# Ids spread across partitions by matmuls, seven one-hots on ACT, and layer 1 summed in steps of two chunks

## The reference

```
e = stack([tbl_f[ids[:, f]] for f in range(40)], axis=1)       # 512 x 40 x 32
z = einsum('bpd,pde,bpe->bp', e[:, iidx], bilinear, e[:, jidx])  # 512 x 780
h = concatenate([z, dense_ctx], axis=1)                          # 512 x 796
h = maximum(h @ W_top1 + b_top1, 0)                              # 512
h = maximum(h @ W_top2 + b_top2, 0)                              # 256
y = h @ W_top3
```

## Time and profile before

| what | value |
|---|---|
| median of 3 runs (lowest, highest) | 208.79 us (207.69, 212.2) |
| the profiled execution | 208.05 us |
| its span, first to last instruction | 206.2 us |
| PE busy | 180.9 us (88%) |
| DVE busy | 152.6 us (74%) |
| POOL busy | 102.9 us (50%) |
| ACT busy | 28.3 us (14%) |
| mean granted clock of PE | 0.992 |

### The profile page before, as it was taken

One profiled execution on the slowest core, in us unless ns is written; L12 is line 12 of the kernel. 1 busy time (PEld: TensorE's weight loads), 2 busy tenths in 40 slices (PEclk: granted clock), 3 DMA queues, 4 the chain that ended last, 5 costly groups with the idle time before them and its releaser, 6 DMA issues.

```text
span 206.2 us, 3399 instructions
## 1 busy us (share of the span) xinstructions
PE 180.9 (88%) x1440; PEld 57.3 (28%) x1440; DVE 152.6 (74%) x153; ACT 28.3 (14%) x40; POOL 102.9 (50%) x110
## 2 busy tenths in 40 slices
PE   0097659569989999999999999999998999999993
PEld 0043213222322232222322333313223223322441
DVE  1588599996779899998458774989693967992502
ACT  2445310100111020011111021100102012001311
POOL 5787787877777777777777777000012020200000
PEclk9999999979999999999999999999999999999999
DMA  6999521130043929140000000000000000000000
GB/s 175 369 368 370 210 67 40 17 97 13 15 116 75 324 27 313 38 153 13 17 14 13 13 13 16 3 0 5 0 0 0 3 0 0 0 3 0 0 0 0
DMA packets 8039, 14.95 MB, mean 72 GB/s; under 512 B 2117, under 2 KB 4553, under 8 KB 8025
## 3 DMA queue, kind: packets, MB, share of 16 engines
q1 hardware_dynamic: 4952, 13.16, 18.8%
q0 software_dynamic: 3072, 1.58, 4.3%
HBM read 14.73 MB, written 0.00 MB: 71 GB/s over the span
## 4 chain that ended last, share of the span: by engine, by line
PE 65%; DVE 4%; issue 2%; DVEq 0%
PE ps_t L589 23%; PE ps_z L603 20%; PE ps_x L630 9%; PE ps_t L583 3%; DVE prod L519 3%; PE ps_t L640 3%; PE ps_t L616 2%; PE ps_x L565 2%; PE ps_x L616 1%; DVE prod L529 0%; PE ps_z L649 0%; DVE prod L532 0%; DVEq L518 0%; DVEq L528 0%
## 5 line engine op out<-in xcount | busy, mean ns | idle before, releaser
L519 DVE TENSOR_TENSOR prod<-ps_t,xt 128x1024 f32<-128x1024 f32 x100 | 115.2, 1215 | 30.1 <-PE ps_t L589 24.7
L426 POOL DMA_INDIRECT emb<-tbl,idx x96 | 96.7, 1007 | 30.1 <-issue 28.7
L589 PE MATMUL ps_t<-xt,w_sb 32*128 32x512 f32 x360 | 59.1, 640 | 0.0
L603 PE MATMUL ps_z<-prod,ones 128*32 128x512 f32 x400 | 53.1, 604 | 0.4 <-DVE prod L519 0.4
L589 PEld LDWEIGHTS ps_t<-xt,w_sb 32*128 32x128 f32 x360 | 20.2, 183 | 33.6 <-issue 23.3
L431 POOL TENSOR_TENSOR late_z<-late_z,tbl_oh 128x512 f32<-128x512 f32 x4 | 5.1, 1277 | 42.9 <-ACT tbl_oh L459 42.9
L482 DVE TENSOR_SCALAR hot<-ids,ramp 128x2048 bf16<-128x2048 f16 x34 | 23.7, 750 | 3.4 <-ACT ids L443 2.1
L553 PE MATMUL ps_x<-hot,tbl_oh 125*32 125x512 bf16 x72 | 8.7, 463 | 13.5 <-DVE hot L482 13.5
L630 PE MATMUL ps_x<-late_z,late_w 128*128 128x512 f32 x40 | 19.3, 613 | 0.0
L603 PEld LDWEIGHTS ps_z<-prod,ones 128*32 128x32 f32 x400 | 8.0, 108 | 39.2 <-issue 29.3
L583 PE MATMUL ps_t<-xt,w_sb 32*32 32x512 f32 x160 | 11.5, 634 | 2.7 <-ACT xt L448 1.9
(11 more groups left out here) (44 smaller groups left out, 68.3 us busy)
## 6 DMA issues: line engine op xcount, KB each, us to landing
late_z<-ids_oh SPq DMA_DIRECT2D x8, 512.0 KB, 7.3
tbl_oh<-small_tables SPq DMA_DIRECT2D x3, 512.0 KB, 6.0
emb<-tbl,idx POOLq DMA_INDIRECT x96, 2.3
late_w<-w SPq DMA_DIRECT2D x1, 1024.0 KB, 7.4
late_w<-w SPq DMA_DIRECT2D x1, 768.0 KB, 6.8
w_sb<-w_pairs SPq DMA_DIRECT2D x1, 704.0 KB, 4.0
tbl_oh<-small_tables SPq DMA_DIRECT2D x1, 640.0 KB, 9.3
w_sb<-w_pairs SPq DMA_DIRECT2D x1, 640.0 KB, 3.9
```

The lines of the kernel that those rows point to most:

```text
L426: nc.gpsimd.indirect_dma_start(emb[:, n % E_RING, t, u * D:(u + 1) * D], None, tables[field], bass.IndirectOffsetOnAxis(ap=idx[:, at:at + ...
L519: nc.vector.tensor_tensor(prod[:, g % PROD_RING, :].rearrange("p (i b) -> p i b", i=2), ps_t[PAIR[g]][:, :].rearrange("p (i b) -> p i b", ...
L589: last = nc.tensor.matmul(o, w_sb[s * D:(s + 1) * D, at:at + P], xt[s * D:(s + 1) * D, kk, :], start=True, stop=True)
L603: last = nc.tensor.matmul(ps_z[q * D:(q + 1) * D, :], ones[:, v * D:(v + 1) * D], prod[:, t // 2 % PROD_RING, t % 2 * B:(t % 2 + 1) * B], ...
```

## The change

1. The sixteen rows of ids are loaded once as 16 x 512 int32. DVE turns them to fp16 (`ids_few`) and builds `to_all`, sixteen matrices of 16 x 128 of which the f-th has ones in row f. PE multiplies: `to_all[f]` by `ids_few` puts row f into all 128 partitions of `ps_t`. Sixteen matmuls, two to a PSUM pair, eight pairs, ring of three; ACT copies each pair (128 x 1024) to fp16. The eight broadcasting transfers and their ring are gone.
2. Seven of the 34 one-hots, listed in `ON_ACT`, are made by ACT as relu(1 - |id - row|), two activations of 128 x 2048 each, into a ring of two of their own, one ahead of PE. DVE makes the other 27. The split of block 3's table moves one chunk earlier, to chunk (2, 3).
3. `EARLY` has three passes of two chunks each, 0-1, 2-3 and 4-5, after groups 26 to 40, 56 to 76 and 88 to 99; `LATE` is chunk 6 alone, in PSUM pairs `ps_t`. POOL adds the second and the third pass.

```
+ON_ACT = [(1, 6), (2, 1), (2, 4), (2, 7), (3, 1), (3, 4), (3, 7)]
-EARLY = [((0, 1, 2), (40, 44, 50, 54)), ((3, 4), (72, 78, 84, 88))]
-LATE = [(5, 0), (5, 1), (5, 2), (5, 3), (6, 0), (6, 1), (6, 2), (6, 3)]
+EARLY = [((0, 1), (26, 30, 34, 40)), ((2, 3), (56, 62, 68, 76)), ((4, 5), (88, 92, 96, 99))]
+LATE = [(6, 0), (6, 1), (6, 2), (6, 3)]
...
-            load_small_ids(0)
-            load_small_ids(1)
...
+            sp.dma_start(ids_raw[:, :], ids_oh_rows).then_inc(ids_raw_in, 16)
             sp.dma_start(idx[:, :], ids).then_inc(ids_in, 16)
...
+            def one_hot(n):
+                j, c = ACT_HOTS[n]
+                wait_slot(act, ACT_HOTS, n, ACT_RING, hot_used_act)
+                o = hot_act[:, n % ACT_RING, :, :]
+                at = OH_FIRST[j] + c
+                nc.scalar.activation(o, ids_oh[:, j, :, :], ACT.Abs, bias=neg_ramp[:, at:at + 1]).then_inc(distance_made, 1)
+                act.wait_ge(distance_made, n + 1)
+                nc.scalar.activation(o, o, ACT.Relu, bias=1.0, scale=-1.0).then_inc(hot_made_act, 1)
...
+            for h in range(2 * len(OH_BLOCKS)):
+                act.wait_ge(ids_spread, h + 1)
+                nc.scalar.activation(ids_oh[:, h // 2, h % 2 * 2:h % 2 * 2 + 2, :].rearrange("p f b -> p (f b)"),
+                                     ps_t[h % 3][:, :], ACT.Copy).then_inc(ids_oh_made, 1)
+            act.wait_ge(ids_oh_made, 2 * len(OH_BLOCKS))
+            one_hot(0)
             for what, k in STEPS:
+                if what == "hot" and k in ACT_HOTS and ACT_HOTS.index(k) + 1 < len(ACT_HOTS):
+                    one_hot(ACT_HOTS.index(k) + 1)
...
+            for h in range(2 * len(OH_BLOCKS)):
+                if h >= 3:
+                    pe.wait_ge(ids_oh_made, h - 2)
+                for f in range(2):
+                    last = nc.tensor.matmul(ps_t[h % 3][:, f * B:(f + 1) * B], to_all[:, 2 * h + f, :], ids_few[:, :],
+                                            start=True, stop=True)
+                last.then_inc(ids_spread, 1)
```

More of the change, by code:

```diff
@@ L193, with slot_free @@
 assert sorted(HOTS) == [(j, c) for j in range(len(OH_BLOCKS)) for c in range(OH_CHUNKS[j])]
+DVE_HOTS = [h for h in HOTS if h not in ON_ACT]
+ACT_HOTS = [h for h in HOTS if h in ON_ACT]
 def is_last_hot(h):
     return h[1] == OH_CHUNKS[h[0]] - 1
-def slot_free(n):
-    if n < HOT_RING:
+def slot_free(hots, n, ring):
+    if n < ring:
         return None, 0
-    h = HOTS[n - HOT_RING]
-    return ("block", OH_BLOCKS[h[0]]) if is_last_hot(h) else ("used", len([i for i in HOTS[:n - HOT_RING + 1]
+    h = hots[n - ring]
+    return ("block", OH_BLOCKS[h[0]]) if is_last_hot(h) else ("used", len([i for i in hots[:n - ring + 1]
                                                                              if not is_last_hot(i)]))
@@ L318, in dlrm_tower @@
         ps_block = {k: ps_z[:, :] if bank == "ps_z" else ps_t[2][:, 0:B] for k, bank in BANK_OF.items()}
-        ps_late = [ps_x[:, :], ps_t[PAIR[NG - 3]][:, 0:B], ps_t[PAIR[NG - 3]][:, B:2 * B], ps_t[PAIR[NG - 2]][:, 0:B]]
+        ps_late = [ps_t[PAIR[NG - 3 + m // 2]][:, m % 2 * B:(m % 2 + 1) * B] for m in range(M1)]
         ps_h2 = [ps_t[PAIR[NG - 1]][:, m * B:(m + 1) * B] for m in range(M2)]
@@ L351, in dlrm_tower, with wait_slot @@
         block = ctx.enter_context(nc.Block())
+        def wait_slot(engine, hots, n, ring, used):
+            what, count = slot_free(hots, n, ring)
+            if what == "block":
+                engine.wait_ge(transposed, count + 1)
+            elif what == "used":
+                engine.wait_ge(used, count)
         def upper_halves(words):
@@ L458, in _ @@
                     if unit >= M1:
-                        nc.scalar.activation(h1_more[:, m, :], ps_x[:, :], ACT.Copy).then_inc(h1_kept, 1)
+                        nc.scalar.activation(h1_more[:, unit - M1, :], ps_x[:, :], ACT.Copy).then_inc(h1_kept, 1)
                     else:
@@ L501, in _ @@
             split_table(0)
-            for n in range(HOT_RING - 1):
+            for n in range(DVE_RING - 1):
                 one_hot(n)
@@ L540, in _ @@
                     j, c = k
-                    n = HOTS.index(k)
+                    if k in ACT_HOTS:
+                        n = ACT_HOTS.index(k)
+                        hot, made, used = hot_act[0:OH_P, n % ACT_RING, :, :], hot_made_act, hot_used_act
+                    else:
+                        n = DVE_HOTS.index(k)
+                        hot, made, used = hot_dve[0:OH_P, n % DVE_RING, :, :], hot_made_dve, hot_used_dve
                     bank = ps_block.get(OH_BLOCKS[j], ps_x[:, :])
@@ L553, in _ @@
                             last = nc.tensor.matmul(bank[s * D:(s + 1) * D, :], values[:, s * D:(s + 1) * D],
[L554 removed]
+                                                    hot[:, s, :],
                                                     start=(c == 0 and part == 0), stop=(is_last_hot(k) and part == 2))
[L556 removed]
+                    last.then_inc(transposed if is_last_hot(k) else used, 1)
                 elif what == "transpose" and k not in OH_BLOCKS:
```

109 lines of the change are left out of this document (53 added, 56 removed).

## The result

The kernel after takes 201.84 us (median of four executions, 200.72 to 202.65) against 208.31 for the kernel before beside it (207.69 to 212.2): the ratio is 0.970, with a 95% interval from 0.964 to 0.975, faster by 3.0%. The ratios and intervals here are not quotients of the medians: they leave out executions over 1.5% above the fastest of their kernel, such as the one of 212.2 us. The forecast was 202.6 us in a range from 200.3 to 206.5, and faster. The profiled execution took 201.93 us with a span of 200.1; before it was 208.05 and 206.2.

A forecast was written before the change was run, and what follows sets the result against it. Bound by a 58 us ramp no engine fills, then PE's matmul queue. Span 206.2 - 6.8 (group 9 earlier) + 1.0 (clock) + 0.36 (layer 1) = 200.8; with 1.85 around it 202.6 us, range 200.3 to 206.5.

The forecast's parts named there:

- ACT's chain: Ramp, blocks 2 and 3: ACT's one-hots and copies in order, 24.6 to 45.9 us, put group 9 at 51.3, -6.8 us.
- the microsecond for the clock: Ramp: 1.0 us added for PE's late clock rise and the fall ahead of block 3 together, between 0 and 3.8.
- ACT's one-hots: Ramp: each one-hot, two activations and the wait between them, takes 4.0 us on ACT, bounds 3.8 and 4.3.
- The start: Before the first chunk: `to_all` 2.27 us, ids 0.70; PE reaches the chunks at 11.4 to 11.8 us, about 1 us later.
- The clock's rise: PE in block 0: from 1.2 to 2.4 GHz by 14 us, since PE has work from 4.65 us on.
- Its fall: PE behind the wait ahead of block 3: 3.8 us at half clock, 1.9 lost, 0.6 covered, so 1.3 us.
- Layer 1: Units among the groups and late matmuls: same 28 matmuls in new places, four terms summing to +0.36 us.
- the other four terms: Layer 1: more starts +0.76, transpose 9's wait gone -0.79, last multiply's wait gone -0.41, uncovered copy at the end +0.80 us.
- a pure wait: Ramp before group 0: 3.7 us waiting for ids that block 0 does not need, its copy standing behind ACT's last piece.
- The rival that the ids were not what held the ramp: Ramp: group 9 gains only DVE's share, seven comparisons, 4.8 us; 205.6 us; chance 0.26 jointly with late rise and dearer one-hots.

## Why the prediction was right, and where it was not

**The sum was right, in part by luck:** 200.8 us of span forecast, 200.1 measured. The order of the waits and ACT's chain were as forecast. Most of the dates held: group 0 at 20.05 (19.6), block 2's copy done at 38.03 (37.9), ACT's last one-hot at 45.69 (45.9), group 9 at 52.06 (52.3 with the microsecond for the clock). ACT's one-hots took 1992 and 1912 ns, a pair 3.84 (4.0).

**The start was mis-sized.** `to_all` took 1.23 us, not the 2.27 worked out from the subtractions, and the ids 0.41, not 0.70:

```profile
1.50 1.23 DVE L517 CAST to_all<-ident 16x2048 f16<-16x2048 f32 x1 [1.50 <-POOL ident L421]
2.66 0.41 DVE L520 CAST ids_few<-ids_raw 16x512 f16<-16x512 int32 x1
```

The Trainium skill's 1227 ns ("VectorE: DVE Perf Modes", section "The perf-mode tier table") was the better price. With ACT's copies at 0.93 us a step in place of 1.06, PE came to the first chunk at 10.13: 0.5 us earlier than before, where I had it 1 us later.

**The clock's rise** came when I said in this profile, by 14 us (in four of the other six with 16 rows it was later), but not for the reason given, that PE works from the start: the spreading matmuls of 16 rows did not bring it, as the run with 128 rows shows. So the 1.4 us won at the start went into chunks at 1.28 us: the first four chunks took 4.3 us (10.13 to 14.40), where the sum had 2.6. That group 0 still came within half a microsecond of its date is two errors that cancel. **Its fall** in block 3 came where I put it, at 1.16 us (1.3).

**Layer 1** was put at +0.36 us and measured at -0.04. The chain shows the term that I left out:

```profile
96.99 1.91 PE ps_x L669 x4
98.90 1.07 PE ps_t L634 x8
99.97 1.00 PE ps_z L648 x8
```

A pair of groups right behind a unit takes 1.07 us and not 1.27. The next one often takes 1.45, but not where another unit or a transpose stands ahead of it; over the queue 19 pairs take 1.07, where it was 17, and the groups' matmuls from group 9 to layer 2 take 59.42 us, where it was 59.81. That is the 0.4; the other four terms are near their rows (the wait for the copy ahead of the late matmuls is 0.81, as forecast 0.80).

**What the sum could not show is who earned it.** The prediction gave each edit a share of one chain, as if shares added. At one fall each, in profiled executions, group 9 moved by 3.08 us for ids that come in order, by 1.46 for ACT's one-hots alone, and by 6.06 for the whole change, which has early ids (by PE) and the one-hots. The ids are worth what the prediction read in the earlier trace rows, a pure wait; but they also free ACT 11 us earlier, and only then can ACT relieve DVE. The rival that the ids were not what held the ramp (205.6) is refuted by the kernel with the ids in order, though the time of the ids alone, 206.9, looks like it: there a second fall of the clock takes most of the gain back. That a shorter ramp may bring more falls stood in no rival. One kernel was not run: the ids in order, by transfers, together with ACT's one-hots. So it is open how much of the gain needs the spreading by PE, and how much a better order on ACT would have given.

## What to carry to other kernels

In a ramp that alternates between engines, test edits together and alone: here two that gain 0.4 to 1% each by themselves gain 3% together, because one frees the engine that the other needs, and because each alone mostly meets a second fall of the clock (37 of 42 executions with early ids, 6 of 10 with ACT's one-hots) that the two together never did (none of after's four). Read the granted clock of every execution beside its time before concluding that an engine has swallowed a gain, but know that it doesn't show the first rise; that is seen in the steps of a profile. And ask what a matmul does for the clock before it is made small: where PE had time to spare, rows of zeros were the cheapest 2 to 3 us.

## What the hardware showed

- PE busy without a hole for 6.9 us with matmuls of 16 rows and 512 columns was still at 1.2 GHz, and rose only behind chunks of 125 rows, at 13.2 to 15.6 us in seven profiles. With 128 rows, and holes of 0.3 us, it was at 2.4 GHz by 9.55 us in three. The granted clock in the rows reads 1.00 in either stretch; the level shows in the steps, 1.28 or 0.66 us a chunk.
- The same wait of 2.35 us was followed by a fall (0.60 over 4 us) in one execution and by none in another. A fall cost 1.2 to 2.6 us, by place.
- Two activations of 2048 elements on ACT, of which the second reads what the first writes, step by 3.84 us; DVE needs 0.68 for the same (2.73 for four in a row). An engine over five times slower still took off 5 us with seven of them, about half of it the second fall, because it was idle.
